# A 3x3 local-attention block: near-key scores in column tiles, P turned on VectorE and placed by DMAs

## The chip, the cores and the metric

The kernel runs on one core of one Trainium2 chip. Times are device microseconds of that core. The kernel before takes 500.1 us, the median of three runs (498.7 to 500.71).

## The reference

```python
x_new = x + w_up2 @ gelu(w_up1 @ depthwise_conv3x3(x))     # 128 -> 384 -> 256 -> 128 channels, with biases
q, k, v = split(w_qkv @ x_new + b_qkv)
scores = stack([(q * shift(k, dy, dx)).sum(-1) for dy, dx in 3x3]) / sqrt(128)   # zero-padded borders
h_attn = sum_i softmax(scores)[i] * shift(v, dy_i, dx_i)
out = x_new + h_attn
```

There are 16 images of 32 x 32 pixels with 128 channels, all in float32. Beyond the border k and v are zero, but the zero keys still take part in the softmax.

## The kernel before

Channels lie on the 128 partitions, and pixels along the free dimension: 1024 per image. Within a row the 32 columns are stored in another order (`place`), which the masks take into account.

The first part of each image is the convolution. The depthwise 3x3 filter and the first 1x1 product are merged into one 3x3 product, computed in a transformed domain. Each image has 12 *units* (`unit`, L340): six transformed positions for each of two halves of the 256 hidden channels. A unit is nine matmuls of 128 x 128 by 256 columns (L359), since operands are split into a high and a low part. VectorE puts the units' results together again (`combine`, `combine_y`, `finish_y`), ScalarE applies the gelu, and `up` (L365) makes the second 1x1 product.

The second part is the attention. The 1024 queries of an image are cut into eight tiles of 128, four rows of the image each. A tile's queries see keys in six rows, that is 192 keys (`WINDOW`); a bf16 product with an identity (L397) writes a mask of 0 or -1e30 into PSUM first, and the product q x h (L401) is added. `scores(n, j)` does two tiles into one PSUM bank, so there are four groups per image. `row_max` (L762) adds five columns for the zero keys and takes the maximum; `exp` (L585) on ScalarE writes P and its row sums; `sums` takes the reciprocal, `normalise` on GpSimd multiplies.

The product with v needs P with the keys on the partitions (`pt`). For the middle 128 of the 192 keys, TensorE transposes four tiles at a time (`transpose_p`, L406) into PSUM and ScalarE copies them to `pt` (`take_pt`, L579). For the 32 keys above and below, VectorE transposes 32 x 32 blocks straight into `pt` (`edges`, L781). Then `values` (L420) multiplies, five products for each half of the image, and `add_h` adds x_new; the sum is stored.

The order is written out by hand: each engine has a `body(n, ...)` that runs the convolution of image n and the attention of image n-1, one after the other in program order, with semaphores between engines. Bodies 0 and 1 fill the pipeline, bodies 2 to 15 are the steady ones, body 16 has no convolution and ends with `last_attention`. On TensorE a body is: unit 0, `transpose_p` of the second half and `values` of the first half of the attention before, unit 1, `values` of the second half, units 2 and 3, `up` twice, units 4 and 5, the projections, unit 6, `scores` 0 and 1, unit 7, `scores` 2, unit 8, `scores` 3, units 9 to 11, `transpose_p` of the first half. SP issues the loads and stores in one queue, each behind its wait: planes of image n+2, rows of image n+1, then the two stores.

## Time and profile before

| | |
|---|---|
| median of three runs | 500.1 us |
| the profiled execution | 498.68 us |
| its span | 496.9 us |
| TensorE busy | 445.7 us, 90% of the span |
| VectorE busy | 356.3 us, 72% |
| ScalarE busy | 230.5 us, 46% |
| GpSimd busy | 194.6 us, 39% |
| DMA, mean over the span | 59 GB/s |

The span is the time from the first to the last instruction on the core; the execution's own time is a little longer. Busy shares are averages over the span. PE is TensorE, PEld its weight loads, DVE is VectorE, ACT is ScalarE, POOL is GpSimd, SP the engine that issues the transfers. An f32 matmul shows as two instructions.

### The profile page before, as it was taken

The page shows a single profiled execution, that of the slowest core. Times are in us where ns is not written, and L with a number is a line of the kernel's source. Part 1 is how long each engine was busy: PE and PEld are TensorE (multiplying, and loading weights), DVE is VectorE, ACT ScalarE, POOL GpSimd, SP SyncE. Part 2 cuts the span into 40 slices and gives each one's busy share as a digit, 9 for nine tenths or more (in the row PEclk, how much of TensorE's full clock was granted, in tenths as well). Part 3 has the DMA queues.
Part 4 walks back from the last instruction along what each step waited for, and adds up shares of the span by engine and source line. Part 5 has one row for each costly group of instructions (what it writes and reads, how often), then busy time and mean ns, then how long its engine had stood idle before and what let it go on. Part 6 is the DMA issues. An engine that isn't in the chain of part 4 may idle for free.

```text
span 496.9 us, 8443 instructions
## 1 busy us (share of the span) xinstructions
PE 445.7 (90%) x2964; PEld 390.7 (79%) x2964; DVE 356.3 (72%) x728; ACT 230.5 (46%) x491; POOL 194.6 (39%) x154
## 2 busy tenths in 40 slices
PE   1558899999999999999999999999999999999984
PEld 1547588787979788787979788797979888797953
DVE  5997669677685958677685958677685958664644
ACT  2443164453627354453626444453736444461633
POOL 3565435344441525344451526344351526320201
PEclk9999899999999999999999999999999999999999
DMA  8101020303103040402104040402204020201011
GB/s 278 65 0 58 0 100 1 140 2 97 46 13 130 2 142 0 140 0 79 62 3 138 0 140 0 140 0 61 79 0 140 0 84 0 86 2 42 1 44 43
DMA packets 11509, 29.31 MB, mean 59 GB/s; under 512 B 2400, under 2 KB 3168, under 8 KB 11488
## 3 DMA queue, kind: packets, MB, share of 16 engines
q1 hardware_dynamic: 10784, 29.03, 17.4%
q8 instruction: 12, 0.20, 0.2%
q10 hardware_dynamic: 704, 0.02, 0.1%
q14 instruction: 9, 0.07, 0.1%
HBM read 20.65 MB, written 8.39 MB: 58 GB/s over the span
## 4 chain that ended last, share of the span: by engine, by line
PE 61%; DVE 21%; issue 10%; ACT 4%; DMA 1%; DVEq 1%; POOLq 0%; POOL 0%; SPq 0%; ACTq 0%
PE m_ps L359 24%; PE work L372 11%; PE s_ps L401 8%; PE work L431 6%; PE work L378 5%; PE work L383 5%; ACT p_sb L589 3%; DVE y L737 3%; DVE y L740 3%; PE s_ps L397 2%; DVE ps_sb L726 2%; DVE negmax L772 2%; DVE pt L792 2%; DVE o_sb L699 1%; DVE y L736 1%
## 5 line engine op out<-in xcount | busy, mean ns | idle before, releaser
L359 PE MATMUL m_ps<-thi,whi 128*128 128x256 f32 x576 | 187.6, 326 | 14.0 <-POOL wlo L927 6.1
L359 PE MATMUL m_ps<-tlo,whi 128*128 128x256 f32 x576 | 164.2, 285 | 0.0
L359 PE MATMUL m_ps<-thi,wlo 128*128 128x256 f32 x576 | 164.1, 285 | 0.0
L359 PEld LDWEIGHTS m_ps<-thi,whi 128*128 128x128 f32 x576 | 111.3, 193 | 22.5 <-issue 15.1
L918 POOL TENSOR_TENSOR p_sb<-p_sb,rsum 128x768 f32<-128x768 f32 x31 | 45.5, 1468 | 192.7 <-DVE rsum L779 192.7
L359 PEld LDWEIGHTS m_ps<-tlo,whi 128*128 128x128 f32 x576 | 111.6, 194 | 7.2 <-issue 7.2
L359 PEld LDWEIGHTS m_ps<-thi,wlo 128*128 128x128 f32 x576 | 111.4, 193 | 0.0
L911 POOL TENSOR_TENSOR tlo<-t,thi 128x1088 fp32r<-128x1088 f32 (+1 forms) x32 | 61.7, 1948 | 46.1 <-ACT thi L528 46.1
L589 ACT ACTIVATE p_sb<-s_ps,negmax 128x197 f32<-128x197 f32 x124 | 51.4, 423 | 37.6 <-DVE negmax L772 37.6
L606 ACT ACTIVATE q_sb<-work,bq_s 128x512 f32<-128x512 f32 x32 | 22.0, 688 | 100.2 <-PE work L378 100.1
L431 PE MATMUL work<-pt,v_sb 128*128 128x160 f32 (+2 forms) x320 | 50.5, 305 | 17.3 <-DVE pt L792 15.8
L431 PEld LDWEIGHTS work<-pt,v_sb 128*128 128x128 f32 x320 | 47.0, 190 | 20.3 <-issue 20.3
L758 DVE TENSOR_TENSOR v_sb<-work,bv 128x256 f32<-128x256 f32 x62 | 26.1, 421 | 45.2 <-PE work L383 44.9
L372 PE MATMUL work<-hid,w2T 128*128 128x512 f32 x120 | 55.7, 608 | 2.0 <-ACT hid L544 2.0
L544 ACT ACTIVATE hid<-y,b1eff 128x1024 f32<-128x1024 f32 x32 | 36.6, 1144 | 36.9 <-DVE y L750 30.9
L401 PE MATMUL s_ps<-h_around,q_sb 128*128 128x192 f32 x248 | 50.4, 326 | 0.0
L528 ACT CAST thi<-t 128x1088 fp32r<-128x1088 f32 (+1 forms) x32 | 26.3, 870 | 43.6 <-DVE t L677 43.6
L401 PEld LDWEIGHTS s_ps<-h_around,q_sb 128*128 128x128 f32 x248 | 42.2, 191 | 1.4
L372 PEld LDWEIGHTS work<-hid,w2T 128*128 128x128 f32 x120 | 22.2, 194 | 24.7 <-issue 24.7
L821 DVE SCALAR_TENSOR_TENSOR h_around<-work,b,xr 128x512 f32<-128x512 f32 x30 | 22.5, 751 | 20.7 <-PE work L372 20.7
L772 DVE TENSOR_REDUCE negmax<-s_ps 128x2 f32<-128x394 f32 x62 | 35.2, 568 | 2.1
L383 PE MATMUL work<-wvT,h_around 128*128 128x129 f32 x248 | 35.3, 275 | 0.9 <-DVE h_around L821 0.9
(110 smaller groups left out, 665.6 us busy)
## 6 DMA issues: line engine op xcount, KB each, us to landing
xp<-x_planes SPq DMA_DIRECT2D x16, 680.0 KB, 5.6
xr<-x_rows SPq DMA_DIRECT2D x16, 512.0 KB, 4.0
out<-o_sb SPq DMA_DIRECT2D x32, 256.0 KB, 4.1
w1T<-w SPq DMA_DIRECT2D x1, 384.0 KB, 3.2
mask_bf<-masks SPq DMA_DIRECT2D x1, 192.0 KB, 4.0
w2T<-w SPq DMA_DIRECT2D x1, 128.0 KB, 4.9
wqk_in<-w_qk SPq DMA_DIRECT2D x1, 128.0 KB, 4.8
ident<-identity SPq DMA_DIRECT2D x1, 64.0 KB, 4.8
```

Source lines behind the costliest of these rows:

```text
L359: last = pe.matmul(m_ps[:, b, col:col + S], a[:, j, dy, half * P:(half + 1) * P], c[:, par, T_PLACE[j], dy * WIN:dy * WIN + S], start=(s = ...
L372: last = pe.matmul(up_bank(n, c), w2T[:, half * C:(half + 1) * C], hid[:, half, c * CH:(c + 1) * CH], start=(half == 0), stop=(half == 1))
L383: last = pe.matmul(v_bank(n, part)[:, u * VT:(u + 1) * VT], h[:, i * P:(i + 1) * P], wvT[:, :], start=True, stop=True)
L401: last = pe.matmul(s[:, u, 0:WINDOW], q_sb[:, i * P:(i + 1) * P], h_around[:, i * P:i * P + WINDOW], start=False, stop=(u == 1), skip_grou ...
L431: last = pe.matmul(work[:, g, (first - g * half) * W:(end - g * half) * W], v_sb[:, i, :], pt[:, i, (first - above) * W:(end - above) * W] ...
L528: nc.scalar.copy(thi[:, par, part, :], t[:, part, :]).then_inc(thi_done, 1)
L544: nc.scalar.activation(hid[:, half, :].rearrange("p (r k s) -> p k r s", k=K4, s=WIN), y[:, half, :, :].rearrange("p k (r s) -> p k r s", ...
L589: nc.scalar.activation(p_sb[:, i, 0:KEYS], s_bank(n, i // 2)[:, u:u + KEYS], ACT.Exp, bias=negmax[:, i:i + 1], accum_out=p_sum[:, i:i + 1] ...
L758: nc.vector.tensor_tensor(v_sb[:, first:end, :], sums[:, :, 0:C], bv[:, :].unsqueeze(1).to_broadcast([P, len(tiles), C]), ALU.add).then_in ...
L772: nc.vector.tensor_reduce(negmax[:, pair], s[:, :, 0:KEYS], AX.X, ALU.max, negate=True).then_inc(rmax_done, 1)
L911: nc.gpsimd.tensor_tensor(tlo[:, par, part, :], t[:, part, :], thi[:, par, part, :].bitcast(F32), ALU.subtract).then_inc(tlo_done, 1)
L918: nc.gpsimd.tensor_tensor(p_sb[:, tiles, 0:WINDOW], p_sb[:, tiles, 0:WINDOW], rsum[:, tiles].unsqueeze(2).to_broadcast([P, 4, WINDOW]), AL ...
```

## The change

The scores of a query are now computed only against the 96 keys (`NEAR`) in its own row and the rows above and below it. `scores(n, g)` does four tiles, and in each the four query rows are separate products: 32 queries as weights, 96 keys as moving columns, written to partitions 32 x row to 32 x row + 31. Four tiles of 128 columns share a PSUM bank, so an image has two groups instead of four, each with one mask product.

P has its near keys at the same columns in every row. `turn_p` transposes all 32 x 32 blocks of half an image with one VectorE instruction into a new buffer `ptc`. Twelve DMAs for each half, issued by SP (`move_p`), copy the blocks from `ptc` to their partitions in `pt`: source 32 partitions x up to 4 tiles x 32 floats each. `transpose_p` on TensorE and `take_pt` on ScalarE are gone, and so is the float32 identity with its load. `values` waits for the DMAs and stands one unit later: the first half behind unit 1, the second behind unit 2. On VectorE the two turns stand behind `combine(n, 1)` and behind `combine_y(n, 1)`. The maximum, the exponentials and the normalising cover 101 or 96 columns per tile instead of 197 or 192.

```diff
+            def move_p(n, g):
+
+                sp.wait_ge(ptc_done, n * 2 + (g - 1))
+                if from_image(n, 2):
+                    sp.wait_ge(o_ready, n * 2 + (g - 3))
+                for row in range(TR):
+                    for dk in range(3):
+                        shift, near = divmod(row + dk - 1, TR)
+                        first, end = max(4 * g, -shift), min(4 * g + 4, T - shift)
+                        col = (near + 2 - dk) * W
+                        sp.dma_start(pt[near * W:(near + 1) * W, first + shift:end + shift, col:col + W],
+                                     ptc[row * W:(row + 1) * W, first:end, dk * W:(dk + 1) * W]).then_inc(
+                                         pt_moved[g], 16)
+
             def body(n, par, conv, attn, store, more):
...
                 if store:
                     store_out(n)
+                if attn:
+                    move_p(n, 0)
+                    move_p(n, 1)
...
-            def scores(n, j):
-                if is_last(n) and j >= 2:
-                    if j == 3:
-
-                        pe.wait_ge(z_done, n * 4 - 2)
-                elif j >= 2 or from_image(n, 2):
-
-                    pe.wait_ge(p_done, n * 8 + (2 * j - 10))
-                s = s_bank(n, j).rearrange("p (a b) -> p a b", a=2)
-                kinds = 0 if j == 0 else 2 if j == T // 2 - 1 else 1
-                pe.matmul(s[:, :, 0:WINDOW], ident_bf[:, :], mask_bf[:, kinds:kinds + 2, :], start=True, stop=False,
-                          skip_group_check=True)
-                for u in range(2):
-                    i = 2 * j + u
-                    last = pe.matmul(s[:, u, 0:WINDOW], q_sb[:, i * P:(i + 1) * P],
-                                     h_around[:, i * P:i * P + WINDOW], start=False, stop=(u == 1),
-                                     skip_group_check=True)
+            def scores(n, g):
+                if from_image(n, 2):
+
+                    pe.wait_ge(p_done, n * 8 + (4 * g - 12))
+                s = s_bank(g)[:, :, 0:NEAR]
+                pe.matmul(s, ident_bf[:, :], mask_bf[:, g:g + 4, :], start=True, stop=False, skip_group_check=True)
+                for u in range(4):
+                    for row in range(TR):
+                        q = ((4 * g + u) * TR + row) * W
+                        last = pe.matmul(s[row * W:(row + 1) * W, u, :], q_sb[:, q:q + W], h_around[:, q:q + NEAR],
+                                         start=False, stop=(u == 3 and row == TR - 1), skip_group_check=True)
                 last.then_inc(s_ready, 1)
 
-            def transpose_p(n, g):
-                if is_last(n) and g == 1:
-                    pe.wait_ge(pn_last_done, 1)
-                else:
-                    pe.wait_ge(pn_done, n * 2 + (g - 1))
-
-                if is_last(n):
-                    pe.wait_ge(z_done, n * 4 - 3 if g == 0 else n * 4)
-                else:
-                    pe.wait_ge(z_done, n * 4 + (0 if g == 0 else -2))
-                for u in range(4):
-                    last = pe.transpose(work[:, 1 + g, u * P:(u + 1) * P], p_sb[:, 4 * g + u, W:W + P], ident[:, :])
-                last.then_inc(pt_ready, 1)
-
             def values(n, g):
 
 
                 pe.wait_ge(v_done, n * 4 - 4)
-                pe.wait_ge(pt_done, n * 2 + (g - 3))
-                pe.wait_ge(edges_done, n * 4 + (2 * g - 6))
+                pe.wait_ge(z_done, n * 4 - 4)
+                pe.wait_ge(pt_moved[g], n * MOVED - MOVED)
...
                     small_weights()
                 units(0)
-                if store:
-                    transpose_p(n - 1, 1)
-                    values(n, 0)
                 units(1)
                 if store:
+                    values(n, 0)
+                units(2)
+                if store:
                     values(n, 1)
-                units(2)
                 units(3)
...
                 if attn:
                     pe.wait_ge(z_done, n * 4 - 3)
                     project_v(n, 3)
-                    scores(n, 2)
-                units(8)
-                if attn:
-                    scores(n, 3)
-                units(9, 10, 11)
-                if attn:
-                    transpose_p(n, 0)
+                units(8, 9, 10, 11)
 
...
-            def take_pt(n, g):
-                act.wait_ge(pt_ready, n * 2 + (g - 1))
-                nc.scalar.copy(pt[:, 4 * g:4 * g + 4, W:W + P],
-                               work[:, 1 + g, :].rearrange("p (t q) -> p t q", t=4)).then_inc(pt_done, 1)
-
             def body(n, par, conv, attn, store, more):
                 def exp(i):
-                    if i % 2 == 0:
-                        act.wait_ge(rmax_done, n * 4 + (i // 2 - 3))
-                    u = i % 2 * STEP
-                    nc.scalar.activation(p_sb[:, i, 0:KEYS], s_bank(n, i // 2)[:, u:u + KEYS], ACT.Exp,
+                    if i % 4 == 0:
+                        act.wait_ge(rmax_done, n * 2 + (i // 4 - 1))
+                        if from_image(n, 2):
+                            act.wait_ge(ptc_done, n * 2 + (i // 4 - 3))
+                    nc.scalar.activation(p_sb[:, i, 0:KEYS], s_bank(i // 4)[:, i % 4, 0:KEYS], ACT.Exp,
                                          bias=negmax[:, i:i + 1], accum_out=p_sum[:, i:i + 1]).then_inc(p_done, 1)
 
-                if store:
...
-            def row_max(n, j):
-
-                pair = slice(2 * j, 2 * j + 2)
-                s = s_bank(n, j).rearrange("p (a b) -> p a b", a=2)
-                z = v_bank(n, j)[:, 0:2 * VT].rearrange("p (t c) -> p t c", c=VT)[:, :, C:VT]
-                dve.wait_ge(v_ready, n * 4 + (j - 3))
-                dve.wait_ge(s_ready, n * 4 + (j - 3))
-                nc.vector.tensor_tensor(s[:, :, WINDOW:KEYS], z.to_broadcast([P, 2, NZ]), z_base[:, pair, :],
-                                        ALU.add).then_inc(z_done, 1)
-                dve.wait_ge(z_done, n * 4 + (j - 3))
-                nc.vector.tensor_reduce(negmax[:, pair], s[:, :, 0:KEYS], AX.X, ALU.max,
+            def row_max(n, g):
+
+                s = s_bank(g)
+                dve.wait_ge(s_ready, n * 2 + (g - 1))
+                for j in (2 * g, 2 * g + 1):
+                    z = v_bank(n, j)[:, 0:2 * VT].rearrange("p (t c) -> p t c", c=VT)[:, :, C:VT]
+                    dve.wait_ge(v_ready, n * 4 + (j - 3))
+                    nc.vector.tensor_tensor(s[:, 2 * j - 4 * g:2 * j - 4 * g + 2, NEAR:KEYS],
+                                            z.to_broadcast([P, 2, NZ]), z_base[:, 2 * j:2 * j + 2, :],
+                                            ALU.add).then_inc(z_done, 1)
+                dve.wait_ge(z_done, n * 4 + (2 * g - 2))
+                nc.vector.tensor_reduce(negmax[:, 4 * g:4 * g + 4], s[:, :, 0:KEYS], AX.X, ALU.max,
...
-            def edges(n, g):
+            def turn_p(n, g):
 
                 if is_last(n) and g == 1:
                     dve.wait_ge(pn_last_done, 1)
                 else:
                     dve.wait_ge(pn_done, n * 2 + (g - 1))
-                first, end = 4 * g, 4 * g + 4
-                a = max(first, 1)
-                nc.vector.transpose(pt[P - W:P, a - 1:end - 1, P + W:WINDOW],
-                                    p_sb[0:W, a:end, 0:W]).then_inc(edges_done, 1)
-                e = min(end, T - 1)
-                nc.vector.transpose(pt[0:W, first + 1:e + 1, 0:W],
-                                    p_sb[P - W:P, first:e, P + W:WINDOW]).then_inc(edges_done, 1)
+                if from_image(n, 2):
+                    dve.wait_ge(pt_moved[g], n * MOVED - MOVED)
+                tiles = slice(4 * g, 4 * g + 4)
+                nc.vector.transpose(ptc[:, tiles, :], p_sb[:, tiles, 0:NEAR]).then_inc(ptc_done, 1)
 
...
                     row_max(n, 0)
-                    row_max(n, 1)
                     if not is_last(n):
                         take_v(n, 3)
-                if attn:
-                    row_max(n, 2)
+                    row_max(n, 1)
                     sums(n, 0)
-                    row_max(n, 3)
                 if is_last(n):
-                    edges(n, 0)
+                    turn_p(n, 0)
                     sums(n, 1)
                     normalise_last(n)
-                    edges(n, 1)
+                    turn_p(n, 1)
                     add_h(n + 1, 0)
                     add_h(n + 1, 1)
                     return
-                if attn:
-                    sums(n, 1)
-                    edges(n, 0)
                 if conv:
                     combine(n, 1)
+                if attn:
+                    turn_p(n, 0)
+                    sums(n, 1)
+                if conv:
                     combine_y(n, 1)
+                if attn:
+                    turn_p(n, 1)
                 if conv:
                     finish_y(n, 1)
-                if attn:
-                    edges(n, 1)
 
             steady(dve, body)
```

Left out are the sizes (`NEAR = 3 * W`, `KEYS = NEAR + NZ`, `STEP = P`, `MOVED = TR * 3 * 16`), the masks for 96 keys, the renamed semaphores, the same order in `last_attention`, and `normalise` over `NEAR` columns.

## Rows read from the trace of the kernel before

**Rows 1.** The page: busy time of TensorE and others; the chain by engine.
```profile
PE 445.7 (90%) x2964; PEld 390.7 (79%) x2964; DVE 356.3 (72%) x728; ACT 230.5 (46%) x491; POOL 194.6 (39%) x154
PE 61%; DVE 21%; issue 10%; ACT 4%; DMA 1%; DVEq 1%; POOLq 0%; POOL 0%; SPq 0%; ACTq 0%
```

**Rows 2.** Timeline of SP: start, duration (us), queue, line, transfer; two successive images.
```profile
203.60 0.35 SPq L277 DMA_DIRECT2D xr<-x_rows  x1
...
231.64 0.35 SPq L277 DMA_DIRECT2D xr<-x_rows  x1
```

**Rows 3.** Timeline of TensorE in a steady image: start, duration until the last ends, line.
```profile
208.72 0.33 PE L397 MATMUL s_ps<-mask_bf,ident_bf 128*128 128x384 bf16 x1
208.88 0.81 PE L401 MATMUL s_ps<-h_around,q_sb 128*128 128x192 f32 x4
209.53 0.33 PE L397 MATMUL s_ps<-mask_bf,ident_bf 128*128 128x384 bf16 x1
...
217.74 0.60 PE L417 MATMUL work<-ident,p_sb 128*128 128x128 f32 x4
218.10 0.36 PE L359 MATMUL m_ps<-thi,whi 128*128 128x256 f32 x1
...
223.49 1.65 PE L431 MATMUL work<-pt,v_sb 128*128 128x32 f32 x10 [1.19 <-DVE pt L792]
224.87 0.39 PE L359 MATMUL m_ps<-thi,whi 128*128 128x256 f32 x1
...
227.09 3.60 PE L372 MATMUL work<-hid,w2T 128*128 128x512 f32 x8
```

**Rows 4.** Timeline of VectorE, the same image, from `combine` to `finish_y`.
```profile
217.45 0.69 DVE L726 TENSOR_TENSOR ps_sb<-m,m_ps 128x512 f32<-128x512 f32 x1
...
218.66 1.33 DVE L736 TENSOR_TENSOR y<-ps_sb 128x256 f32<-128x256 f32 x1
...
222.03 0.67 DVE L750 TENSOR_TENSOR y<-y,m_ps 128x512 f32<-128x512 f32 x1
```

**Rows 5.** Groups by shape: VectorE's transposes, busy us and mean ns of one.
```profile
L792 DVE STREAM_TRANSPOSE pt<-p_sb 32x128 f32<-32x128 f32 x16 | 4.9, 303 | 0.5
...
L792 DVE STREAM_TRANSPOSE pt<-p_sb 32x96 f32<-32x96 f32 x16 | 4.3, 269 | 0.5
```

**Rows 6.** Timeline of SP at the start, where issues follow without a wait.
```profile
5.50 0.43 SPq L270 DMA_DIRECT2D zeros<-zero_keys  x1
5.97 0.43 SPq L273 DMA_DIRECT2D xp<-x_planes  x1
```

**Rows 7.** The page: DMA queues; issues with KB each and us to landing.
```profile
q1 hardware_dynamic: 10784, 29.03, 17.4%
q10 hardware_dynamic: 704, 0.02, 0.1%
xr<-x_rows SPq DMA_DIRECT2D x16, 512.0 KB, 4.0
...
wp<-w_perc ACTq DMA_DIRECT2D x1, 13.5 KB, 3.4
```

**Rows 8.** Timeline of TensorE in body 1; stretch 58 to 60, clock third from last.
```profile
56.17 5.37 PE L372 MATMUL work<-hid,w2T 128*128 128x512 f32 x8 [2.05 <-ACT hid L544]
...
58.00:60.00 2.00, 2.00 (x3) 0.68 (x2) 0.75 (x1) 0.00 (x0) 0.00 (x0) 0.50 0.00 0
```

**Rows 9.** Timeline of TensorE in body 16: after the last unit, the last attention.
```profile
469.11 1.25 PE L417 MATMUL work<-ident,p_sb 128*128 128x128 f32 x8
...
474.27 3.60 PE L372 MATMUL m_ps<-hid,w2T 128*128 128x512 f32 x8
...
484.98 0.81 PE L401 MATMUL m_ps<-h_around,q_sb 128*128 128x192 f32 x4
...
491.97 1.66 PE L431 MATMUL work<-pt,v_sb 128*128 128x32 f32 x10 [0.72 <-issue]
```

**Rows 10.** Waits: engine and line, for whom, us in total, times, longest.
```profile
DVE p_sb L690 <- DMA ident<-identity: 1.4, 1, 1.4
```

More of the change, by code:

```diff
@@ L211, in build @@
         rsum_done = sem("rsum_done")
-        edges_done = sem("edges_done")
+        ptc_done = sem("ptc_done")
+        pt_moved = [sem(f"pt_moved{i}") for i in range(2)]
         pn_last_done = sem("pn_last_done")
@@ L280, in _ @@
             load_planes(0, 0)
-            sp.dma_start(ident[:, :], ident_c).then_inc(first_in, 16)
             load(w2T[:, :], w2_c)
@@ L554, in prime_gelu @@
             def prime_gelu():
[L556 to L558 removed]
+                nc.scalar.activation(primer[:, :], w1T[:, 0, 0:1], ACT.Gelu).then_inc(primed, 1)
+            act.wait_ge(first_in, 16)
             prime_gelu()
```

62 lines of the change are left out of this document (25 added, 37 removed).

## The prediction

> **What bounds the kernel now.** I read the page's busy shares first: TensorE is busy for 90% of the span, and the chain that ended last runs 61% through it [rows 1]. The DMA issues put a clock on the loop: one load of `xr` per image, 203.60 and 231.64, so an image takes 28.04 us [rows 2]. Then TensorE's own timeline over one image [rows 3]. The reader is to see one dense sequence with a single idle stretch, 1.19 us ahead of `values(n, 1)` at 223.49, ended by VectorE. TensorE does its work in the order of the program, so an image costs 28.04 - 1.19 = 26.85 us of its work plus whatever it stands still for. Work taken off TensorE counts in full; so does every wait put into its queue. VectorE comes second: around the turn of the image it runs `combine` (1.21 us from 217.45 to 218.66) and `combine_y` (3.37 us from 218.66 to 222.03) back to back [rows 4]. All other engines have room.
>
> I count from the end of unit 9 (call it t=0), the last thing that `combine(n, 1)` needs. A unit is (227.09 - 224.87)/2 = 1.11 us [rows 3].
>
> **TensorE's work.** Removed: eight transposes, 0.36 us for four (217.74 to 218.10), 0.7 us per image; two of four mask products, 0.16 us each (208.72 to 208.88), 0.3 us [rows 3]. Changed: a score group of two tiles, four instructions of 192 columns, took 0.65 us (208.88 to 209.53), 2.6 us per image. An f32 product is two instructions here (x4 for two), at 0.65/4 = 0.163 us for 192 columns, 0.85 ns a column. The new ones are 8 tiles x 4 query rows = 32 products, 64 instructions with 64 weight loads, of 96 columns. Lower bound: the four column strips of 32 run wholly beside each other, 16 x 96 x 0.85 ns = 1.3 us. Upper bound: the pitch of the 256-column convolution instructions, 1.11/9 = 0.123 us, 64 x 0.123 = 7.9 us. One after the other by columns it is 64 x 0.082 = 5.2 us. The nearest row for short instructions, each with its own weights, is the transposes: 128 columns in 0.36/4 = 0.09 us, though they take one pass. I take 0.09: 5.8 us, that is +3.2 us per image. Work per image: 26.85 - 0.7 - 0.3 + 3.2 = 29.05 us.
>
> The Trainium skill, "TensorEngine Tiling (Array Packing)", Theoretical Speedup, gives up to 4x for a small dimension of at most 32; its section Instruction Overhead adds that each matmul carries about 60 cycles whatever its length. No row of this trace shows a column-tiled product; by the first the scores would come near the lower bound above, and that is the first rival.
>
> **The way of P.** Before, four transposes on TensorE, a ScalarE copy and short VectorE transposes; the worst of it was the 1.19 us wait. After, for each half g: VectorE's `turn_p`, then 12 DMAs from SP, then `values`. Step by step:
> - `turn_p(n, 0)` stands behind `combine(n, 1)`: 0.2 us from unit 9 to the start, 1.2 for `combine` [rows 4]. The turn has 384 columns; 96 take 269 ns and 128 take 303 [rows 5], 1.06 ns a column, so 0.6 us. SP starts at t = 2.1 with 0.1 for the semaphore.
> - SP issues one DMA per 0.47 us when nothing holds it: 5.50 to 5.97 [rows 6]. Twelve are 5.6 us, twenty-four 11.3 us. Bounds of the pitch: 0.35 us (the shortest issue, at 203.60, [rows 2]) and 0.6 us for a pattern with one dimension more (an estimate: 0.47 and a quarter).
> - Landing after the issue of the last: `xr`, 512 KB, takes 4.0 us, the 13.5 KB of `wp` 3.4 us [rows 7]. Queue q1 moved 29.03 MB in 17.4% of 16 x 496.9 us, 21 MB/ms per engine, so 512 KB over 16 engines are 1.5 us and 2.5 us are left as latency. I take 2.5 for 16 KB from SBUF to SBUF; bounds 1.0 and 3.4.
> - The packets: a copy has 32 partitions x 4 tiles = 128 runs of 128 bytes, 12 copies 96 per engine. They stay under the 5.6 us of issue if one takes under 59 ns. Rows: q10, 704 small packets in 0.1% of 7950 us, about 11 ns each; q1, 2.7 KB packets, 1383/10784 = 128 ns each [rows 7]. The small ones are the nearer; I count nothing.
>
> So P of half 0 is there at t = 2.1 + 11 x 0.47 + 2.5 = 9.8. TensorE arrives after units 10, 11, 0 and 1 at t = 4.4: it waits 5.4 us. Half 1 is issued behind half 0 on SP: `combine_y` and `turn_p(n, 1)` are done at about t = 6.2, while SP is busy to t = 7.8, so SP sets it. P of half 1: 2.1 + 23 x 0.47 + 2.5 = 15.4. TensorE has done `values(n+1, 0)` (1.38 us, 223.49 to 224.87, [rows 3]) and unit 2 by 12.3: it waits another 3.1 us. `values(n+1, 1)` ends at t = 16.8. The later place of `values` by one unit (1.11 us) is far less than the 8.5 us. Behind the wait in TensorE's queue stand unit 3, `up`, and all of the next image; VectorE's `add_h` waits for `values`, and with it the next transform, but that has room.
>
> The period is 16.8 plus TensorE's work from there to the next unit 9: 29.05 less five units (5.55) and two `values` (2.76) = 20.75. Sum 37.5 us.
>
> **The clock.** After a standstill of 2.05 us the granted clock fell to 0.50 of full (1.2 instead of 2.4 GHz) in 58 to 60 us, and the eight products of `up` took 5.37 us there against 3.60 in a steady image, +1.8 us [rows 3, 8]. The steady 1.19 us never showed it. With stalls of 5.4 and 3.1 us a low stretch is likely; what falls between the two stalls is covered by the second. I take half of one, 0.9 us; bounds 0 and 3. Period 38.4, +10.4 us per image.
>
> **What is hidden.** The row maximum, the exponentials (101 instead of 197 columns) and normalising (96 instead of 192) get shorter, all ahead of t=0 where TensorE's units cover them: no gain. The ScalarE copies that go were beside other work. SP's `load_planes(n+3)` now stands behind the 24 copies and starts most of a turn later, but what it loads is wanted a whole image on, and a landing is 4 us: nothing. The start: `ident` no longer gates `first_in`; VectorE had waited 1.4 us for it [rows 10]: -1.4.
>
> **Sum.** Image 1 has scores and no `values`: +2.9. Fourteen bodies with both: 14 x 10.4 = +146. Body 16 has no units: before, from unit 11 (469.11) `up` started at 474.27, 5.2 us [rows 9]; now `values(16, 1)` ends at 16.8 - 2.2 = 14.6: +9.4. The last attention: before, 485.6 (484.98 + 0.65) to 493.35, 7.7 us [rows 9]; now SP starts 1.6 us after the last score (the first half's P is ready then), and 1.6 + 10.8 + 2.5 + 1.4 = 16.3: +8.6, and +2.9 for the scores: +11.5. Together -1.4 + 2.9 + 146 + 9.4 + 11.5 = +168. The profiled execution was 498.7 us with a span of 496.9, inside the range of the runs (498.7 to 500.7, median 500.1): 498.7 + 168 = 667 us.
>
> **Rivals.**
> 1. The column strips run abreast. For: they are disjoint quarters of the array; against: each product still needs an instruction and a weight load, and the shortest pitch seen is 0.09. Scores 1.3 us: 4.5 us less per image, 16 images, -72: 595 us. Chance 0.27.
> 2. The DMA engines set the pace: at 128 ns a packet a half takes 12.3 us, not 5.6; per image +13, 667 + 16 x 13 = 880 us; at 80 ns, +4 per image, 730. For: 3072 packets per image where there were 10784/16 = 674; against: q10's 11 ns. Chance 0.08.
> 3. The clock stays low after both stalls: 2 us more per image, 667 + 15 x 2 = 697. Chance 0.10.
> 4. Not slower: the copies are out at once and land early. The period is 17.6 + (score change) + 2.1 + 23p + L + 1.4 with p the pitch and L the landing; it stays under 28.04 only with 23p + L under 6.9 less the score change. With the scores abreast (-1.3) and L = 2.5 that wants p under 0.25 us. With p = 0.1 the period is 24.6 and the time about 498.7 - 15 x 3.4 = 448 us. For: the old issues overlap nothing that shows whether a copy within SBUF is issued faster; against: 0.35 us is the shortest issue of all. Chance 0.05.
>
> The Trainium skill, "DMA: Bandwidth & Descriptors", Issuing engines are not separate DMA queues, says the time the sequencer takes to start a DMA is usually small relative to the DMA itself. That is the fourth rival; this trace shows 0.47 against some 2.5 us for one, and the change makes 24 of them. Its Rules for kernel authors speak against the change: coalesce many small transfers, below 64 KB one pays mostly overhead; a copy here is 16 KB.
>
> **How the numbers follow.** Forecast 0.50, rivals 0.27, 0.08, 0.10, 0.05. The range: rival 1 with no lost clock gives 595 - 15 x 0.9 = 582; the forecast with a pitch of 0.6 (+3 per image) or rival 2's milder form reach 715 to 730. I give 585 to 730. A difference of 0.5% is what the measurement can tell. Only rival 4 is not slower: faster 0.04, same 0.01, slower 0.95.
>
> **What would show it.** TensorE idle ahead of `values` and released by the DMA into `pt`, about 5.4 and 3.1 us per image, some 130 us in all; SP's issues 0.47 apart in blocks of 24; the period 38.4; the score instructions 0.09 apart. Wrong if the copies are issued closer, if the strips overlap, or if the wait is for `turn_p` rather than for SP.

## The result: 1.37 times the time, and the profile after

The changed kernel takes 682.4 us (median of 4 runs, 681.6 to 683.0) where the kernel before took 499.4 us beside it (498.6 to 500.7). The ratio is 1.366, with a 95% interval of 1.362 to 1.370. The profiled execution took 682.2 us with a span of 680.4 us. The forecast was 667 us.

The page, read in the order of [rows 1]: busy time (us, share of the span, instructions), then the chain that ended last by engine, then the costliest wait of the kernel (engine and line, for whom, us in total, times, longest).

```profile
PE 481.8 (71%) x3572; PEld 413.7 (61%) x3572; DVE 321.5 (47%) x664; ACT 199.1 (29%) x459; POOL 175.1 (26%) x154
...
PE 44%; SPq 31%; issue 10%; DMA 4%; DVE 3%; ACT 0%; POOL 0%; POOLq 0%; DVEq 0%
```

```profile
PE work L429 <- DMA pt<-ptc: 167.9, 32, 12.1
```

TensorE's share fell from 90% to 71%, and SP's issuing, which had no part in the chain before, is 31% of it. In the kernel before, `values` also waited, for VectorE's transposes. Its row on the page of the kernel before (busy us, mean ns, then the idle time ahead and what ended most of it):

```profile
L431 PE MATMUL work<-pt,v_sb 128*128 128x160 f32 (+2 forms) x320 | 50.5, 305 | 17.3 <-DVE pt L792 15.8
```

So the idle time ahead of `values` grew by 167.9 - 17.3 = 151 us, most of the loss of 183 us.

SP's timeline over two images (start, duration until the last of the group is issued, transfer), which answers to [rows 2]:

```profile
348.41 15.46 SPq L310 DMA_DIRECT2D pt<-ptc  x24
...
386.99 15.45 SPq L310 DMA_DIRECT2D pt<-ptc  x24
403.11 0.36 SPq L273 DMA_DIRECT2D xp<-x_planes  x1
...
426.89 1.26 SPq L310 DMA_DIRECT2D pt<-ptc  x2
```

The blocks of 24 copies follow each other after 38.58 and 39.90 us by turns (the view ends inside the third block). From image 1 (72.84) to image 15 (622.78) it is 549.94/14 = 39.28 us per image on average, where it was 28.04. One copy is 15.45/24 = 0.644 us of SP's time, while issuing the load of 680 KB behind them takes 0.36.

TensorE's timeline of the same image (start, duration until the last ends, and in brackets the idle time ahead with what ended it), answering to [rows 3]:

```profile
395.96 2.98 PE L429 MATMUL work<-pt,v_sb 128*128 128x160 f32 x10 [6.62 <-DMA pt<-ptc]
398.75 0.56 PE L377 MATMUL m_ps<-thi,whi 128*128 128x256 f32 x1
...
403.76 3.11 PE L429 MATMUL work<-pt,v_sb 128*128 128x32 f32 x10 [3.32 <-DMA pt<-ptc]
406.47 0.61 PE L377 MATMUL m_ps<-thi,whi 128*128 128x256 f32 x1
...
408.59 4.24 PE L390 MATMUL work<-hid,w2T 128*128 128x512 f32 x8
412.26 0.68 PE L377 MATMUL m_ps<-thi,whi 128*128 128x256 f32 x1
...
418.92 0.33 PE L410 MATMUL s_ps<-mask_bf,ident_bf 128*128 128x384 bf16 x1
419.18 0.87 PE L414 MATMUL s_ps<-h_around,q_sb 128*32 128x96 f32 x32
419.98 0.34 PE L410 MATMUL s_ps<-mask_bf,ident_bf 128*128 128x384 bf16 x1
```

Three things stand in it. Both waits are where they were forecast, 6.62 and 3.32 us for 5.4 and 3.1 (this is an image of the longer period). The 32 instructions of a score group take 419.98 - 419.18 = 0.80 us, 0.025 us each. And what follows a wait is slow: `values(n, 0)` takes 398.75 - 395.96 = 2.79 us (1.34 before), `values(n, 1)` 2.71 (1.38), the unit behind it 2.12 (1.11), `up` 3.67 (3.03). The granted clock of these stretches says why (us, busy time of PE, PEld, DVE, ACT and POOL, then the clock, DMA share, GB/s):

```profile
392.00:396.00 4.00, 0.04 (x1) 0.04 (x1) 0.47 (x2) 1.43 (x2) 1.47 (x2) 0.60 0.16 25
396.00:400.00 4.00, 4.00 (x17) 4.00 (x18) 0.93 (x2) 0.00 (x0) 0.00 (x0) 0.55 0.17 27
...
404.00:408.00 4.00, 4.00 (x17) 4.00 (x18) 0.69 (x1) 0.00 (x0) 2.23 (x2) 0.50 0.50 174
408.00:412.00 4.00, 4.00 (x11) 2.21 (x11) 2.04 (x3) 0.00 (x0) 0.00 (x0) 0.77 0.00 0
```

After each of the two standstills TensorE works at the lower level, 1.2 GHz (0.55 and 0.50). VectorE sets the start of the block and not its length: the turn of the first half ends at 386.96, and SP begins at 386.99; the turn of the second half is done at 391.20, about 3.5 us before SP comes to the copies of that half (386.99 + 12 x 0.644 = 394.7). The landing is read from the issues (KB each, us from the start of the issue to the landing), which answers to [rows 7]:

```profile
386.39 0.57 DVE L767 STREAM_TRANSPOSE ptc<-p_sb 128x384 f32<-128x384 f32 x1
...
390.63 0.57 DVE L767 STREAM_TRANSPOSE ptc<-p_sb 128x384 f32<-128x384 f32 x1
```

```profile
pt<-ptc SPq DMA_DIRECT2D x352, 16.0 KB, 1.8
```

### The profile page after: what moved, and what is told of

It is laid out like the page before. It is cut to its first block, busy times and chain, and to the rows that moved or that the text cites. A ratio compares the mean times of both kernels' runs of the same rounds, so it can differ in the third digit from the quotient of the medians.

```text
span 680.4 us, 9913 instructions
## 1 busy us (share of the span) xinstructions
PE 481.8 (71%) x3572; PEld 413.7 (61%) x3572; DVE 321.5 (47%) x664; ACT 199.1 (29%) x459; POOL 175.1 (26%) x154
## 4 chain that ended last, share of the span: by engine, by line
PE 44%; SPq 31%; issue 10%; DMA 4%; DVE 3%; ACT 0%; POOL 0%; POOLq 0%; DVEq 0%
SPq L310 31%; PE m_ps L377 17%; PE work L390 8%; PE work L429 7%; DMA pt<-ptc 4%; PE work L401 4%; PE work L396 4%; PE s_ps L414 4%; DVE ptc L767 1%; PE s_ps L410 1%; DVE ps_sb L702 0%; DVE ru_sb L703 0%; DVE y L713 0%; ACT hid L530 0%; DVE y L718 0%
## 5 line engine op out<-in xcount | busy, mean ns | idle before, releaser
L429 PE MATMUL work<-pt,v_sb 128*128 128x160 f32 (+2 forms) x320 | 95.9, 482 | 167.9 <-DMA pt<-ptc 167.9
L429 PEld LDWEIGHTS work<-pt,v_sb 128*128 128x128 f32 x320 | 88.0, 325 | 173.6 <-issue 105.4
L377 PEld LDWEIGHTS m_ps<-thi,whi 128*128 128x128 f32 x576 | 121.2, 210 | 25.5 <-issue 14.9
L377 PEld LDWEIGHTS m_ps<-tlo,whi 128*128 128x128 f32 x576 | 120.3, 209 | 7.2 <-issue 7.2
L776 DVE TENSOR_TENSOR o_sb<-work,h_around 128x512 f32<-128x512 f32 x32 | 22.1, 692 | 210.7 <-PE work L429 210.7
L377 PEld LDWEIGHTS m_ps<-thi,wlo 128*128 128x128 f32 x576 | 119.4, 207 | 0.0
L890 POOL TENSOR_TENSOR p_sb<-p_sb,rsum 128x384 f32<-128x384 f32 x31 | 27.0, 870 | 324.4 <-DVE rsum L756 324.4
L530 ACT ACTIVATE hid<-y,b1eff 128x1024 f32<-128x1024 f32 x32 | 36.6, 1144 | 71.7 <-DVE y L726 45.9
L571 ACT ACTIVATE p_sb<-s_ps,negmax 128x101 f32<-128x101 f32 x128 | 42.4, 345 | 9.0 <-DVE negmax L749 8.9
L702 DVE TENSOR_TENSOR ps_sb<-m,m_ps 128x512 f32<-128x512 f32 x32 | 22.0, 688 | 31.3 <-PE m_ps L377 24.0
L401 PEld LDWEIGHTS work<-wvT,h_around 128*128 128x128 f32 x248 | 31.7, 191 | 1.7 <-issue 1.7
```

What stands on the lines that cost most here:

```text
L377: last = pe.matmul(m_ps[:, b, col:col + S], a[:, j, dy, half * P:(half + 1) * P], c[:, par, T_PLACE[j], dy * WIN:dy * WIN + S], start=(s = ...
L401: last = pe.matmul(v_bank(n, part)[:, u * VT:(u + 1) * VT], h[:, i * P:(i + 1) * P], wvT[:, :], start=True, stop=True)
L429: last = pe.matmul(work[:, g, (first - g * half) * W:(end - g * half) * W], v_sb[:, i, :], pt[:, i, (first - above) * W:(end - above) * W] ...
L530: nc.scalar.activation(hid[:, half, :].rearrange("p (r k s) -> p k r s", k=K4, s=WIN), y[:, half, :, :].rearrange("p k (r s) -> p k r s", ...
L571: nc.scalar.activation(p_sb[:, i, 0:KEYS], s_bank(i // 4)[:, i % 4, 0:KEYS], ACT.Exp, bias=negmax[:, i:i + 1], accum_out=p_sum[:, i:i + 1] ...
L890: nc.gpsimd.tensor_tensor(p_sb[:, tiles, 0:NEAR], p_sb[:, tiles, 0:NEAR], rsum[:, tiles].unsqueeze(2).to_broadcast([P, 4, NEAR]), ALU.mult ...
```

## The experiments

The theory (A), formed from the trace after: the kernel has become a closed loop through SP. The period is the way from one block of copies to the next: 24 issues, a landing, `values`, and TensorE's work up to unit 9 of the next image; what TensorE does meanwhile is covered. Rivals: the copies' data, not their issue, takes the time (then fewer copies help less, and their shape matters); the extra time is the scores' many instructions; the low clock is as dear as the waits. The "period" is always the mean over the 14 periods from the block of image 1 to that of image 15. Unless an edit is said to keep the computation, it doesn't.

One slip runs through four expectations. Those of `one_copy`, `six_copies`, `two_queues` and `late_values` subtract from a period of 39.9 us, the longer of the two that alternate, and not from the mean of 39.28. That alone makes their totals 14 x 0.62 = 9 us too low.

**1 and 2: how many copies.** `one_copy` leaves out eleven of the twelve copies of each half, `six_copies` six of twelve.

```
-        MOVED = TR * 3 * 16
+        MOVED = 16                      # six_copies: 6 * 16
...
-                for row in range(TR):
-                    for dk in range(3):
+                for row in (1,):         # six_copies: (1, 2)
+                    for dk in (1,):      # six_copies: range(3)
```

> Each half's twelve copies are cut to one (the middle block of row 1); eleven are left out, so most of P is not placed. Theory (SP's issue of the copies sets the end of both waits): P of half 0 at t = 2.0 + 1.8 = 3.8 us after unit 9, before TensorE arrives at 4.4; P of half 1 at turn_p's end 6.2 + 1.9 = 8.1, TensorE there at 6.9, so a wait of 1.2 us. Period 9.5 + 16.5 = 26 us, total 682 - 14 x 13.9 - 2 x 11 = about 465 us. Rival (the landing latency, the turn on VectorE or the low clock make up most of it): the period stays above 33 us, total above 590 us.

> Each half's twelve copies are cut to six (query rows 1 and 2); the other six are left out. Theory (0.644 us of issue for each copy): P of half 1 at 2.0 + 11 x 0.644 + 1.8 = 10.9, period 10.9 + 1.4 + 16.5 = 28.8 us, total 682 - 14 x 11 - 2 x 8 = about 512 us; from six to twelve copies a half costs 12 x 0.644 = 7.7 us per image plus what the clock loses. Rival (one fixed delay, whatever the number): the same total as with one copy, within 1%.

`one_copy`: 473.3 us beside 499.5 for the kernel before (ratio 0.949, 0.941 to 0.956), period 26.27 us. The 682.4 - 473.3 = 209 us between it and the changed kernel, more than the whole loss of 183, are the eleven copies and what they bring on; with a single copy left in each half the rest of the change (scores, `turn_p`, the later `values`) gains 26 us. The expectation, 465, was 8 us too low, which is the slip above. `six_copies`: 545.0 us (ratio 1.093, 1.085 to 1.100), period 30.62; the expectation, 512 with a period of 28.8, was too low by 33 us: 9 by the slip above, and 14 x 1.8 = 25, about the rest, by the period. TensorE of `six_copies`, then SP:

```profile
322.18 2.98 PE L429 MATMUL work<-pt,v_sb 128*128 128x160 f32 x10 [2.77 <-DMA pt<-ptc]
```

```profile
317.06 8.03 SPq L310 DMA_DIRECT2D pt<-ptc  x12
```

The second wait is gone (twelve issues take 8.03 us, with a short gap between the halves), but behind the first, 2.77 us, the clock is already at half, 0.50 in 324 to 328: `values` takes 2.8 us where 1.3 were reckoned, and the other half 1.9. So the time is a matter of the number of copies, and the clock is a price of its own.

**3: what a copy costs.** In `flat_copies` each copy goes into one unbroken stretch per partition (384 bytes in one run instead of four of 128 bytes), so that the packets of the copies fall to a quarter (it is 12 KB, not 16); P lands in wrong places. In `wide_copies` a copy has 128 partitions and 128 bytes from each, the same 16 KB.

```
flat_copies
-   sp.dma_start(pt[near * W:(near + 1) * W, first + shift:end + shift, col:col + W],
-                ptc[row * W:(row + 1) * W, first:end, dk * W:(dk + 1) * W])
+   sp.dma_start(pt[near * W:(near + 1) * W, 5 * g + dk, 0:NEAR],
+                ptc[row * W:(row + 1) * W, 4 * g + dk, :])
wide_copies
+   sp.dma_start(pt[:, 5 * g + dk, row * W:(row + 1) * W],
+                ptc[:, 4 * g + dk, 0:W])
```

> The same 24 copies per image, but each moves one run of 96 floats per partition of one tile (32 runs of 384 bytes, 12 KB) in place of 4 runs of 128 bytes (128 runs, 16 KB); P lands in wrong places. Theory A (the longer issue, 0.644 us against 0.47 at the start of the kernel before, comes from the further dimension or the number of runs): the pitch falls to about 0.47, the period by 23 x 0.17 = 4 us, total about 618 us. Theory B (an issue from SBUF to SBUF or a partial-partition copy costs this whatever its shape): pitch 0.64, total 682 us within 1%.

> The changed kernel with the same 24 copies per image, each now of all 128 partitions and 32 floats of one tile (128 runs of 128 bytes, 16 KB as before); P lands in wrong places. Theory A (an issue costs 0.64 us because only 32 partitions take part): the pitch is 0.47 us, total about 682 - 16 x 4 = 618 us. Theory B (it costs that because source and target are in SBUF, or for the wait state of the queue in a loop): 0.64 us, total 682 us within 1%.

SP of `flat_copies`, then of `wide_copies`:

```profile
344.21 15.09 SPq L310 DMA_DIRECT2D pt<-ptc  x24
```

```profile
346.05 15.28 SPq L310 DMA_DIRECT2D pt<-ptc  x24
```

672.5 us (ratio 1.348, 1.339 to 1.357) and 677.6 us (1.357, 1.351 to 1.363). The pitch is 0.629 and 0.637 us for 0.644. Neither the number of runs nor that of the partitions makes the issue of a copy dearer than the 0.47 us of [rows 6]; the kernels differ by 1.5% and 0.7% from the changed one, and the slightly shorter pitch is over half of that (24 x 0.015 x 16 = 6 of 10 us for the first, 24 x 0.007 x 16 = 3 of 5 for the second). One difference from the loads is left, that source and target both lie in SBUF, but no run had the same copy with one end in HBM: what makes the issue dearer stays open. Rival 2 of the prediction, packets that set the pace, is out.

**4: two queues.** `two_queues` issues every second copy from ScalarE, behind its exponentials, and keeps the computation.

```
+        def move_p(eng, n, g, part):
...
+                    if (row * 3 + dk) % 2 != part:
+                        continue
...
-                    move_p(n, 0)
-                    move_p(n, 1)
+                    move_p(sp, n, 0, 0)     # and move_p(act, n, 0, 1) on ScalarE
+                    move_p(sp, n, 1, 0)     # and move_p(act, n, 1, 1)
```

> The whole computation; of the twelve copies of a half, every second is issued by ScalarE, behind its exponentials, the others by SP. Theory (the time goes into issuing, and each issuing engine has its own): P of half 0 at 2.1 + 5 x 0.644 + 1.8 = 7.1 us after unit 9, P of half 1 at 6.3 + 5 x 0.644 + 1.8 = 11.3, waits of 2.7 and 1.7 us, period 12.7 + 16.5 = 29.2 us, with lost clock up to 30.2: total 682 - 14 x 10 - 2 x 8 = about 525 us. Rival (both engines share what makes the pitch, a descriptor generator or the DMA engines): each queue's pitch doubles to 1.3 us and the total stays at 682 us.

SP and ScalarE of `two_queues`:

```profile
317.29 8.38 SPq L278 DMA_DIRECT2D pt<-ptc  x12
```

```profile
317.30 8.09 ACTq L278 DMA_DIRECT2D pt<-ptc  x12
```

546.8 us (ratio 1.096, 1.087 to 1.105), period 30.57. Twelve copies take 8.38 us on SP and 8.09 on ScalarE, each beside the other, and 8.03 on SP alone in `six_copies`. A shared limit would have doubled the pitch, so the limit is the time of the issuing engine. The time is that of `six_copies` to 2 us, with twice the copies. This is the direct test of the theory: putting half of the issues on another engine, and nothing else, gives back 682.4 - 546.8 = 136 us. It came out 22 us above the expected 525: 9 are the slip above, and the clock behind a wait of 3.10 us is in the rest. From the first `values` to `up` it takes 7.8 us (322.74 to 330.51), for 4.9 in the kernel before without its wait.

**5: the score instructions.** `one_strip` puts all four query rows of a tile into the first 32-column strip.

```
-   last = pe.matmul(s[row * W:(row + 1) * W, u, :], q_sb[:, q:q + W], ...
+   last = pe.matmul(s[0:W, u, :], q_sb[:, q:q + W], ...
```

> All four query rows' products of a tile write the same strip, partitions 0 to 31 (the other strips keep the mask alone, so the scores are not the reference's); number, size and order of the products are unchanged. Theory A (the 0.025 us pitch of the changed kernel's score instructions comes from the four column strips working beside each other): the instructions follow at 96 columns x 0.83 ns = 0.08 us, the 64 take 5.1 instead of 1.6 us, the period grows by 3.5 us, total about 682 + 16 x 3.5 = 738 us. Theory B (short products with short weight loads run at 0.025 us wherever they write): the pitch and the total stay, 682 us within 1%.

TensorE of `one_strip`, a score group and the mask product behind it:

```profile
368.65 2.83 PE L414 MATMUL s_ps<-h_around,q_sb 128*32 128x96 f32 x32
371.41 0.34 PE L410 MATMUL s_ps<-mask_bf,ident_bf 128*128 128x384 bf16 x1
```

745.7 us beside 497.1 (ratio 1.497, 1.491 to 1.504), period 43.37, +4.1 us. The same 32 instructions take 2.76 us, 0.086 us each, where four strips give 0.80. So the strips do run beside each other, weight loads included. And 0.086 is close to what I had forecast from the transposes (0.09), and to the 0.082 that 96 columns give at 0.85 ns: both rows were right for one strip, and wrong for four.

**6: what the clock costs.** `filled_waits` puts bf16 products that nobody reads ahead of the two waits, 34 and 26, about as long as the waits. The computation is kept.

```
                 pe.wait_ge(z_done, n * 4 - 4)
+                for _ in range((34, 26)[g]):
+                    pe.matmul(work[:, 2, 0:4 * NEAR], ident_bf[:, :], mask_bf[:, 0:4, :], start=True, stop=True)
                 pe.wait_ge(pt_moved[g], n * MOVED - MOVED)
```

> The whole computation, and ahead of each wait for the copies TensorE makes products that nobody reads (34 and 26 of 384 columns, bf16, about 5.4 and 4.2 us, short of the waits). Theory (part of the loss is the clock at half speed behind each standstill): the granted clock stays at 1.00, values 1 takes 1.4 in place of 2.7 us, unit 3 1.1 in place of 2.1 and up 3.0 in place of 3.7, 3.0 us per image less: total 682 - 14 x 3.0 - 5 = about 635 us. Rival (the low clock is covered by the waits, or the extra products delay the copies): 682 us or more.

TensorE of `filled_waits`, 40 us in one stretch, then its second `values` and `up`:

```profile
380.00:420.00 40.00, 38.19 (x306) 29.68 (x305) 20.05 (x43) 11.66 (x27) 10.33 (x9) 1.00 0.21 55
```

```profile
387.14 1.68 PE L431 MATMUL work<-pt,v_sb 128*128 128x32 f32 x10 [0.73 <-DMA pt<-ptc]
...
389.72 3.60 PE L390 MATMUL work<-hid,w2T 128*128 128x512 f32 x8
```

648.9 us (ratio 1.303, 1.297 to 1.309); period 37.15. The clock is 1.00 throughout, `values` and `up` have their old lengths, and the period is 39.28 - 37.15 = 2.1 us shorter: that is the price of the clock per image. The expectation, 635, took the longer of the two alternating periods as the rule. Only 2.1 of 11.2 us: the waits, not the clock, are the main thing.

**7: a later place for `values`.** `late_values` has units 0 to 5 ahead of both `values` (`add_h` moved accordingly); the computation is kept.

```
-                units(0)
-                units(1)
+                units(0, 1, 2, 3)
                 if store:
+                    units(4, 5)
                     values(n, 0)
-                units(2)
-                if store:
                     values(n, 1)
-                units(3)
```

> The whole computation, copies from SP alone, but both values stand behind unit 5 instead of behind units 1 and 2, unit 6 takes the place of units 4 and 5 behind up, and add_h stands behind the transform. Theory (the way of P, 18.7 us from unit 9, is fixed, and what TensorE does meanwhile is gained): 8 instead of 5 units run beside it, the period is 18.7 + 0.5 + 2.7 + 13.1 + 1.6 = 36.6 us in place of 39.9, total about 682 - 14 x 3.3 = 636 us, still far above the kernel before. Rival (the later values delay add_h, the transform and the next image's chain by as much): 682 us within 1%.

TensorE of `late_values`:

```profile
384.30 3.11 PE L429 MATMUL work<-pt,v_sb 128*128 128x32 f32 x10 [6.19 <-DMA pt<-ptc]
```

648.4 us (ratio 1.302, 1.296 to 1.308), period 36.86 (expected 36.6). Work moved ahead of the waits takes 2.4 us out of the loop and no more, for the block of copies is as long as before. The expectation of the total, 636, was 12 us too low: 14 x 0.26 = 4 by the period, and 9 by the slip above. The two ends of the kernel have no part in it, for 14 x 2.42 = 34 us is the whole of 682.4 - 648.4.

**8, 9 and 10: both, and then the clock.** `late_two_queues` joins experiments 7 and 4 and puts `turn_p(n, 0)` ahead of `combine(n, 1)` and `turn_p(n, 1)` ahead of `combine_y(n, 1)`; `between_units` has units 4 and 5 between the two `values`; `between_units_filled_end` also has products that nobody reads ahead of the waits of body 16 and the last attention, where there is no other work. All keep the computation.

```
late_two_queues -> between_units
-                    units(4, 5)
                     values(n, 0)
+                    units(4, 5)
                     values(n, 1)
between_units -> between_units_filled_end, ahead of the wait in values
+                if isinstance(n, int) and n >= B:
+                    for _ in range(((30, 9), (48, 9))[n - B][g]):
+                        pe.matmul(work[:, 2, 0:4 * NEAR], ident_bf[:, :], mask_bf[:, 0:4, :], start=True, stop=True)
```

> The whole computation: the late values, the copies shared between SP and ScalarE, and the turns one place earlier on VectorE (ahead of combine and ahead of combine_y). Theory: P of half 0 is there some 9.5 us and P of half 1 some 13.5 us after the last score, TensorE arrives at 11.5 and 12.9, so nearly no wait is left; the period is TensorE's work, 26.85 - 0.7 - 0.3 - 1.0 = 24.8 us, with half a microsecond of wait 25.3. Total 499.5 - 14 x 2.7 - 1.4 + about 7 for the last attention = about 467 us, faster than the kernel before. Rival (ScalarE, now holding copies in its queue ahead of the gelu, makes up late): a period near 28 us and about 505 us.

> late_two_queues with values of half 0 moved from behind unit 5 to behind unit 3. Before, unit 4 waited some 1.0 us for finish_y, and values of half 1 then waited 0.3 us for the copies. Theory: the first copies have landed 0.5 us after TensorE gets there, finish_y is done while values 0 runs, and 0.5 us per image is gained: 493.8 - 14 x 0.5 = about 487 us. Rival (the second half's copies set the end either way): 494 us, no change that can be measured.

> between_units, and in body 16 and in the last attention products that nobody reads fill TensorE's waits for the copies (30, 9, 48 and 9 of them). Theory: the clock stays at full speed in these two places, values 0 takes 1.5 in place of 2.9 us, values 1 1.7 in place of 3.1 us, up 0.8 less; the first halves are covered by the wait for the second, so about 1.4 x 2 + 0.8 = 3.6 us are gained against between_units: some 483 us. Rival (the waits cover all of it): the same time within 1 us.

SP and TensorE of `late_two_queues`:

```profile
285.58 8.12 SPq L278 DMA_DIRECT2D pt<-ptc  x12
...
312.09 8.12 SPq L278 DMA_DIRECT2D pt<-ptc  x12
```

```profile
317.57 0.36 PE L378 MATMUL m_ps<-thi,whi 128*128 128x256 f32 x1 [0.98 <-DVE y L732]
...
321.57 1.66 PE L430 MATMUL work<-pt,v_sb 128*128 128x32 f32 x10 [0.34 <-DMA pt<-ptc]
```

`late_two_queues`: 493.8 us beside 497.1 (496.8 to 499.8); its four runs lie at 488.8, 490.7, 497.0 and 497.8, so that the two kernels are not to be told apart; expected 467. In the steady stretch the period is 312.09 - 285.58 = 26.51 us, 1.2 more than I had reckoned from TensorE's work; the mean over the 14 periods is 26.83. A loop is closed even here: `up` to the last score 10.8, from there to the first copy 4.7, issue and landing together 9.5 (312.09 to 321.57), `values` 1.5, together 26.5. Inside this loop the turn of P ahead of `combine` delays `finish_y`, and unit 4 waits 0.98 us for it. `between_units`: 494.5 us beside 498.5 (ratio 0.990, 0.984 to 0.995), expected 487; its rival, no change from 494, is what came. The steady period is 26.51 again (mean 27.10). The wait has only moved:

```profile
296.29 1.60 PE L430 MATMUL work<-pt,v_sb 128*128 128x160 f32 x10 [0.94 <-DMA pt<-ptc]
...
300.32 1.66 PE L430 MATMUL work<-pt,v_sb 128*128 128x32 f32 x10 [0.23 <-DMA pt<-ptc]
```

`between_units_filled_end`: 492.8 us (487.1 to 497.5) beside the same (ratio 0.986, 0.981 to 0.991), expected 483. The medians of these three kernels are closer together than the runs of each, so what filling the end is worth isn't shown. This one is 1.4% ahead of the kernel before. At the steady period it would be ahead by 28.04 - 26.51 = 1.5 us per image, 21 us in 14 images, but its mean period is 27.11, so the loop gives 13 us. The difference lies in a few long periods, of which more below. About half of the 13 us goes again outside these periods, above all at the end, where the last two `values` wait for copies with no other work to cover them: in `late_two_queues` TensorE stands 5.17 us in body 16 and 8.59 in the last attention.

**11: shortening the 4.7 us.** `early_turn` turns the first half's P before the row maximum of the second half, so that the first copy goes out sooner; a one-column exponential behind the gelu has ScalarE load its table early. Otherwise it is `between_units_filled_end`. The computation is kept.

```
+                    nc.scalar.activation(primer[:, :], w1T[:, 0, 0:1], ACT.Exp)...
...
+                        sums(n, 0)
                         take_v(n, 3)
-                    row_max(n, 1)
-                    sums(n, 0)
+                        turn_p(n, 0)
+                        row_max(n, 1)
```

> between_units_filled_end, with a one-column exponential behind the first gelu so that the table is loaded ahead of the row maximum (1.28 us earlier), with sums and turn_p of half 0 ahead of row_max of half 1, and turn_p of half 1 behind combine. In the kernels before it the period was 26.5 us = 10.8 us of TensorE from up to the last score + 4.7 us to the first copy + 7.8 us of issue + 1.8 us of landing + 1.4 us of values, a closed loop. Theory (this loop sets the period): the first copy starts 3.1 instead of 4.7 us after the last score, the period falls to TensorE's own work, 25.0 us, total 492.8 - 14 x 1.5 = about 472 us. Rival (TensorE's own work was the bound and the waits are only its slack): 493 us within 1%.

504.9 us (500.1 to 507.0) beside 499.3 (ratio 1.011, 1.007 to 1.015): slower, against an expected 472. Three views of `early_turn` in two successive images. First SP's timeline:

```profile
265.32 7.92 SPq L278 DMA_DIRECT2D pt<-ptc  x12
273.62 0.35 SPq L288 DMA_DIRECT2D xp<-x_planes  x1
...
293.49 7.93 SPq L278 DMA_DIRECT2D pt<-ptc  x12
302.28 0.35 SPq L288 DMA_DIRECT2D xp<-x_planes  x1
```

ScalarE's last ten copies:

```profile
267.72 6.52 ACTq L278 DMA_DIRECT2D pt<-ptc  x10
...
295.90 6.53 ACTq L278 DMA_DIRECT2D pt<-ptc  x10
```

The chain in the first image (start, us, what), and TensorE's second `values` of the next image, which has no wait:

```profile
273.62 4.13 DMA pt<-ptc
277.89 1.66 PE work L433 x10
```

```profile
303.75 1.66 PE L433 MATMUL work<-pt,v_sb 128*128 128x32 f32 x10
```

The aim was reached: the first copy starts 3.3 us after the last score (290.18 to 293.49) instead of 4.7. What came of it wasn't foreseen. SP's copies are issued by 273.2, and ScalarE, whose copies go out between its exponentials and behind them, begins to issue its last one at 273.62. At that moment SP starts the load of the planes, 680 KB, and the last copy lands 4.13 us after the start of its issue; the others take 1.8 to 2.0. `values(n, 1)` waits 2.31 us for it. In the next image the last issue begins at 301.8, half a microsecond before the load, and there is no wait. The third image is like the first. Periods of 28.2 and 25.9 us follow each other (265.32, 293.49, 319.38), 27.0 on average. The short one shows what the loop could do. That the load slows the copy rests on this coincidence in the traces alone; moving the load was not tried.

The mean of 27.66 us over the 14 periods also holds two long ones, 31.0 and 31.6 us. In the later of the two, TensorE's second `values` and a stretch of 4 us behind its start are

```profile
386.62 3.11 PE L433 MATMUL work<-pt,v_sb 128*128 128x32 f32 x10 [2.72 <-DMA pt<-ptc]
```

```profile
388.00:392.00 4.00, 4.00 (x9) 2.54 (x9) 1.88 (x3) 0.00 (x0) 2.45 (x2) 0.50 0.00 0
```

The wait is 2.72 us instead of 2.31, and behind it the granted clock is 0.50, where it stayed at 1.00 behind the waits of 2.31 and 2.51 us: `up` takes 4.6 us instead of 3.0. The same happens once in `between_units`, in a period of 31.58 us: the load of the planes starts at 107.68, the last copy, issued from 107.61, lands after 4.57 us, TensorE waits 3.67, and the clock is 0.50 in 114 to 116. So both the meeting with the load and the lower clock were already there before `early_turn`, in single images.

## Why the prediction was right, and where its terms were not

The mechanism, the place and the sign were right: TensorE waits for the copies at both `values`, SP's issues set both waits, the sum was 667 for 682. But three terms missed by 4.2, 4.0 and 1.2 us per image, each by more than the whole period did (0.9), and they largely cancelled. That the sum came so close is luck.

- **TensorE's work.** Forecast +3.2 us per image for the scores, at 0.09 us per instruction. Measured 0.025: 64 instructions in 1.6 us for 2.6 before, so -1.0. This is the step of the sum that was mis-sized, by 4.2 us per image. Rival 1's mechanism (strips abreast) is what happens; its 595 us didn't come, as it had the rest of my sum. Two bounds were at hand, 1.3 and 7.9 us, and I took the value of the row that was nearest in kind; its ends held. The Trainium skill, "TensorEngine Tiling (Array Packing)", Theoretical Speedup, has up to 4x for a dimension of at most 32; the trace agrees, with 0.086/0.025 = 3.4. Its section Instruction Overhead has about 60 cycles per matmul, an estimate of 0.025 us at 2.4 GHz. That is the length measured, but a quarter of 0.086 is 0.022, so the agreement doesn't show that such an overhead is the bound.
- **The pitch.** Forecast 0.47 us from [rows 6], measured 0.644: 23 x 0.17 = +4.0 us per image. It lay just above my upper bound of 0.6. The start-up issues were loads; no row showed a copy from SBUF to SBUF.
- **The landing.** Forecast 2.5 us from the start of the last issue, measured 1.8: -0.7.
- **Start and places.** SP's first issue came at t = 2.0 (386.99; forecast 2.1), P of half 0 at t = 10.9 for 9.8, of half 1 at 18.7 for 15.4. The waits of 6.62 and 3.32 us follow.
- **The clock.** Forecast 0.9 us per image within 0 to 3, measured 2.1 (experiment 6). What falls ahead of the second wait is covered, as reckoned. I had half of what is behind it; it is `values(n, 1)`, a unit and part of `up`. In the shorter of the two alternating periods `up` is at full clock again (3.60 us at 369.38), so the truth lay between my forecast and rival 3.
- **Per image** -4.2 + 4.0 - 0.7 + 1.2 = +0.3 by these terms, and the period came out 39.28 for 38.4; 0.6 us is left over. Of this 0.2 are the two mask products, which stand 0.26 us ahead of the strips (418.92 to 419.18) where I had 0.16; the rest no term of mine names.
- **The sum.** Fourteen periods: 14 x (39.28 - 28.04) = 157 us for 146. Body 16: from unit 11 (ends near 623.0) to `up` at 642.46 it is 19.5 us, +14.3 for +9.4. The last attention: from the last score (654.2) to the end of `values` (676.8) 22.6 us, +14.9 for +8.6, with 3.1 us to SP's first copy instead of 1.6. `ident`'s gate: the first `combine` starts at 39.95 instead of 40.92, -1.0 for -1.4. Two images of shorter scores outside the periods, -2. Together 157 + 14.3 + 14.9 - 1.0 - 2 = 183, which is the measured difference.
- **Hidden edits.** Row maxima, exponentials and `load_planes` cost nothing, as forecast. That `load_planes` stands right behind the copies was harmless in this kernel and decisive in `early_turn`.
- **Rivals 2 and 4** are out: the shape of the copies changes their pitch by 1 to 2%, and a quarter of the packets changes the time by 1.5% (experiment 3), and the pitch is 0.64 us.

Body 16 and the last attention, TensorE of the changed kernel, which answer to [rows 9]:

```profile
642.46 5.06 PE L390 MATMUL m_ps<-hid,w2T 128*128 128x512 f32 x8
...
653.36 0.87 PE L414 MATMUL s_ps<-h_around,q_sb 128*32 128x96 f32 x32
666.35 2.95 PE L429 MATMUL work<-pt,v_sb 128*128 128x160 f32 x10 [12.12 <-DMA pt<-ptc]
674.05 3.11 PE L429 MATMUL work<-pt,v_sb 128*128 128x32 f32 x10 [4.76 <-DMA pt<-ptc]
```

## What to carry to other kernels

Replacing work on the busiest engine by DMAs only pays if the issuing engine's time fits between producer and consumer: count the DMAs, multiply by the issue time of that kind of copy, and split them over idle queues before anything else. A short idle time on the engine that bounds the kernel can be paid twice, once as the wait and once as the low clock behind it, so place consumers late enough or keep the engine busy. Once a loop is closed through another engine, a shorter path only pays as far as the next one, and earlier transfers may meet loads that they never met before.

## What the runs showed of the hardware that I had not expected

- Products of f32 (two instructions each) in four 32-column strips run beside each other, with their weight loads: 0.025 us per instruction, 0.086 in a single strip.
- Issuing a copy within SBUF takes 0.60 to 0.62 us and some 0.65 from one to the next, on SP (0.644) as on ScalarE, for 16 KB in 128-byte runs, 12 KB in 384-byte runs or 16 KB over 128 partitions alike (0.63 to 0.65); issuing a load of 680 KB in the same loop takes 0.36. The Trainium skill, "DMA: Bandwidth & Descriptors", Issuing engines are not separate DMA queues, has the issue as usually small relative to the DMA. The trace doesn't agree for these copies: here it is a third of the landing (1.8 us) and, twelve in a row, four times as long.
- ScalarE's issues run beside its own exponentials. ScalarE of `early_turn`, queue and engine:

```profile
294.61 0.61 ACTq L278 DMA_DIRECT2D pt<-ptc  x1
294.67 0.34 ACT L575 ACTIVATE p_sb<-s_ps,negmax 128x101 f32<-128x101 f32 x1
```

- Behind waits of 2.8 to 6.6 us in a loop TensorE was at 1.2 GHz for what came next, 2.1 us per image in the changed kernel. The length of the wait alone doesn't tell: behind 2.31 and 2.51 us in `early_turn` the clock stayed at 1.00, behind 2.72 in the same trace and 2.05 in [rows 8] it fell to 0.50. Products that nobody reads in the wait keep it at 2.4 GHz and win 33.5 us (682.4 to 648.9).
